# Attention outputs kept turned and unnormalised until the out-projection

## The chip, the cores and the metric

The kernel runs on one NeuronCore of a Trainium2 chip. The metric is the device time of one execution in microseconds. TensorE multiplies into PSUM, VectorE (DVE) and ScalarE (ACT) read PSUM and SBUF, GpSimd (POOL) reads SBUF alone, and DMAs are issued by a queue of an engine, here mostly SyncE's (SP), and carried out by 16 DMA engines.

## The reference

x is (4, 2048, 256) in float32. Attention and feed-forward part read the same normalised x:

```python
xn = _layernorm(x)
q, k = rope(xn @ Wq.T), rope(xn @ Wk.T)       # 16 heads of 16
v = xn @ Wv.T
attn = softmax(where(causal, q @ k.T / 4, min))
x = x + (attn @ v).reshape(B, S, D) @ Wo.T + ffn_fp4(xn)
```

The feed-forward part (SwiGLU with inputs and weights rounded to blockwise FP4) is computed in the first stage and already added to x there; the change doesn't touch it.

## The kernel before

Three stages, each a block of its own with a barrier behind it. `norm_ffn_qkv` (to about 868 us) makes q, k and v and stores them in DRAM; its stores of q and k (line 299) go out by halves of heads:

```python
dst = d["qkp"][p, f // 2, :, ds(g, 1), first:first + HEAD // 2].rearrange("h g e a c -> h (g e a) c")
sp.dma_start(dst, parts[:, p, f, :]).then_inc(parts_stored, 16)   # DRAM: 4 x 32 x 512, bf16
```

`attention` runs 16 iterations, one for each group of four heads (HG) and batch. In an iteration there are four blocks of 512 queries (qb). Each block needs the maximum of every row of scores first: tiles of raw scores in PSUM (`max_tile`, L979; VectorE reduces them, L1143 and L1148), whose maxima GpSimd splits into three bf16 parts, TensorE turns (`max_row`), and SP places as extra rows of q. Then come the scores transposed, keys by queries (`scores`, L1002, with the causal mask as a product with identity, L1007), the exponential on ScalarE (`exponentials`, L1071) and the weighing of v (`weigh`, L1022), four heads side by side in `acc`. v has 32 columns a head (VW), 16 of v and one of ones, so that `acc` holds for each head 16 rows of outputs and a row of sums, turned: channels by queries. When a block is complete ScalarE copies `acc` to `acc_sb` (`take_acc`, L1076). An "out" follows: TensorE turns it with four transposes (`out_turn`, L1032) into a slot of the same ring of four PSUM tiles that the maxima use, VectorE takes reciprocals of the sums (L1172) and multiplies (L1175, `normalise`), and SP stores `ot` to `oscr` (L913).

The order of all this is written out: `ORDER` is a string in which s is a step of scores (weighings follow from them), t a tile of maxima, r a placing of a row, o an out. `attention_plan` makes the list from it, and each engine goes through this list and takes what is its own. Tiles of the next iteration run ahead (about half of them), so every iteration but the last has 140 tiles. The loop has two iterations in its body on SP, TensorE and VectorE, one on ScalarE, which loads its table of functions again at the start of each.

`out_projection` handles 16 groups of 512 rows in pairs. SP loads a group by four DMAs, one for each group of heads (L1240, 128 partitions x 4 x 64 elements); for each tile of 128 rows TensorE turns the outputs (two transposes, L1269), ScalarE copies them to `attT` (L1295), TensorE multiplies with Wo (L1277, float32, two instructions a product) and VectorE adds x (L1311). SP stores a group of y (L1252), behind which the next loads stand in its queue.

Of the kernel before, what the change touches and what calls it, by code (L numbers as in the profile page):

```python
# [26 lines left out]
P = 128  # L27
# [25 lines left out]
OUTW = HG * HEAD  # L53
OT = GT * OUTW

LEAD = 0.52
WEIGH_AT, WEIGH_STEPS = 3, 2
ORDER = ("stsststtsttssststststsssstststsstssrtsssttstssotststsstsststststtstsststssststststssttsstsssstst"
         "stsststsssststssttsotsststsstttsststsststttsstsssststsstttststssssststststssttsssstrtstssttstsst"
         "stsssstssttstssssrtsssttstsststsoststsststststtsststtstsssstsstststttssssssstststtrsststsssststs"  # L60
         "ttssttstsstssstsstttstsststssststsstststtststsssssstttssssto")
# [737 lines left out]
def ring_places(plan, more):  # L799


    uses = [e for e in plan if e[0] in ("tile", "row", "out") and (more or e[0] == "out" or not e[-1])]
    return {e: n for n, e in enumerate(uses)}


def slot_free(it, n, per_iteration, slots):
# [6 lines left out]
    return it * per_iteration + last - per_iteration + 1 + slots  # L813


def attention(nc, d, identf):
# [21 lines left out]
    with ExitStack() as ctx:  # L838
# [18 lines left out]
        acc_sb = sb("acc_sb", [P, GROUP])  # L857
        recip = sb("recip", [P, GT * HG])
        ot = sb("ot", [P, 2, GT * HG, HEAD])
# [17 lines left out]
        dve_links = sem("dve_links")  # L877
# [4 lines left out]
        out_stored = [sem("out_stored0"), sem("out_stored1")]  # L882
        sp_passed = sem("sp_passed2")
# [3 lines left out]
        def _(sp):  # L887
# [20 lines left out]
            def store(it, more, e):  # L908
                n, _ = place(it, more, e)
                qb = e[1]  # L910
                await_on(sp, sp_passed, tile_taken, n + 1 + TILE_SLOTS)
                dst = d["oscr"].rearrange("h g p c -> (h g) p c")[ds(it * QB + qb, 1)]
                sp.dma_start(dst.rearrange("a p c -> (a p) c"),  # L913
                             ot[:, qb % 2].rearrange("p t e -> p (t e)")).then_inc(out_stored[qb % 2], 16)
# [13 lines left out]
            def iteration(it, par, more):  # L928

                last = QB - 1  # L930
                for e in plan:
                    if e[0] == "row" and (more or not e[-1]):
                        place_row(it, (par + e[-1]) % 2, more, e)
                    elif e[0] == "out":
                        store(it, more, e)
# [19 lines left out]

            await_on(sp, sp_passed, out_stored[0], ITERS * QB // 2 * 16 + 1)
# [3 lines left out]
        def _(pe):  # L960
# [66 lines left out]
            def out_turn(it, more, e):  # L1027

                pe.wait_ge(acc_taken, it * QB + e[1] + 2)
                bank = tile_slot(it, more, e)  # L1030
                for t in range(GT):
                    mm = nc.tensor.transpose(bank[:, t * P:(t + 1) * P], acc_sb[:, t * P:(t + 1) * P], identf[:])  # L1032
# [334 lines left out]
```

## Time and profile before

| | us |
|---|---|
| median of 3 runs | 2679.75 (2678.06 to 2680.13) |
| the profiled execution | 2682.65, its span 2680.5 |
| TensorE busy, whole span | 2496.1 (93%) |
| VectorE busy | 2267.2 (85%) |
| ScalarE busy | 1629.3 (61%) |
| GpSimd busy | 80.7 (3%) |
| mean granted TensorE clock | 0.971 |

Busy is the union of an engine's instructions; a product counts until its last result, also while the next one already streams, so shares of TensorE near 100% say that there are no gaps, not that it works at its peak. A clock of 1.00 is 2.4 GHz, 0.5 is 1.2 GHz. Attention fills the span from about 868 to 2594 us, the out-projection the rest.

### The profile page before, as it was taken

What the parts mean: (1) busy time and instruction counts of PE and PEld (TensorE: products, weight loads), DVE (VectorE), ACT (ScalarE), POOL (GpSimd) and SP (SyncE); (2) the same over time, 40 slices, a digit from 0 to 9 for tenths busy, and PEclk for the clock granted to TensorE, in tenths of its full rate; (3) what the DMA queues carried; (4) which work ended last, traced back from release to release, by engine and by line L of the source; (5) the groups of instructions that cost most, each with busy time, mean ns of one, the idle gap of its engine ahead of it and who ended that gap; (6) DMA issues with size and microseconds to landing.
All of it is one profiled execution on the core that took longest, in us unless ns stands there. A gap on an engine that the chain in (4) does not pass through costs nothing. (4 is left out here: it accounts for less than half of the span.)

```text
span 2680.5 us, 55917 instructions
## 1 busy us (share of the span) xinstructions
PE 2496.1 (93%) x14690; PEld 1211.5 (45%) x14690; DVE 2267.2 (85%) x4941; ACT 1629.3 (61%) x3323; POOL 80.7 (3%) x263
## 2 busy tenths in 40 slices
PE   3699999999998699999999999999999999999979
PEld 2355655555555144344344444344444443433337
DVE  6989889998897888889889888988988988988803
ACT  2354454544543067777777777777777777767752
POOL 0000000000000200000000000000000000000000
PEclk8899999999999599999999999999999999999999
DMA  5022112211221402112112022121121121110017
GB/s 182 34 69 70 56 62 70 70 51 68 69 70 55 122 26 64 31 51 65 27 55 63 25 59 58 30 59 41 47 58 33 51 62 28 52 53 6 7 40 215
DMA packets 174760, 157.83 MB, mean 59 GB/s; under 512 B 53360, under 2 KB 153456, under 8 KB 174576
## 3 DMA queue, kind: packets, MB, share of 16 engines
q1 hardware_dynamic: 174576, 155.39, 19.5%
q8 instruction: 114, 1.87, 0.3%
q14 instruction: 70, 0.57, 0.1%
HBM read 95.81 MB, written 58.72 MB: 58 GB/s over the span
## 5 line engine op out<-in xcount | busy, mean ns | idle before, releaser
L1071 ACT ACTIVATE prob<-score 128x512 f32<-128x512 f32 (+3 forms) x2560 | 1158.7, 542 | 494.5 <-PE score L1007 273.1
L1143 DVE TENSOR_REDUCE top<-tile 128x1 f32<-128x512 f32 x1536 | 957.1, 682 | 109.1 <-PE tile L979 102.5
L1002 PE MATMUL score<-qs,ks 99*128 99x512 bf16 (+3 forms) x2560 | 811.6, 351 | 17.1 <-DMA qs<-row 9.9
L979 PE MATMUL tile<-ks,qs 96*128 96x512 bf16 (+3 forms) x2560 | 786.8, 357 | 30.6 <-POOL ks L1095 22.3
L1022 PE MATMUL acc<-prob,vs 128*32 128x512 f32 (+3 forms) x5120 | 537.9, 535 | 0.0
L1148 DVE CUSTOM_DVE_ANT_0 tile<-tile,mask 128x128 f32<-128x128 f32 (+3 forms) x1024 | 471.6, 519 | 59.7 <-PE tile L979 43.6
L1002 PEld LDWEIGHTS score<-qs,ks 99*128 99x128 bf16 x2560 | 246.7, 97 | 405.5 <-ACT prob L1071 204.9
L979 PEld LDWEIGHTS tile<-ks,qs 96*128 96x128 bf16 x2560 | 236.4, 98 | 327.2 <-DVE top L1143 100.9
L361 PE MATMUL gu<-wguT,xT 128*128 128x512 f32 (+1 forms) x768 | 314.4, 563 | 20.4 <-DVE hid L669 20.4
L1022 PEld LDWEIGHTS acc<-prob,vs 128*32 128x32 f32 x5120 | 130.3, 109 | 242.9 <-issue 139.3
L361 PEld LDWEIGHTS gu<-wguT,xT 128*128 128x128 f32 x768 | 145.0, 192 | 167.6 <-issue 124.8
L1007 PE MATMUL score<-identb,maskb 128*128 128x128 bf16 x1024 | 214.5, 221 | 3.4 <-issue 3.4
L397 PE MATMUL misc<-wdT,hT 128*128 128x256 f32 x768 | 183.9, 391 | 1.3 <-ACT hT L462 1.3
L397 PEld LDWEIGHTS misc<-wdT,hT 128*128 128x128 f32 x768 | 147.9, 196 | 32.7 <-issue 11.3
L1148 DVE DVE_READ_ACCUMULATOR2_ANT top<- 128x1 f32 x1024 | 143.4, 140 | 0.0
L385 PE MATMUL misc<-xT,wqkvT_sb 128*128 128x512 f32 x256 | 118.7, 607 | 7.6 <-ACT xT L462 7.6
L1007 PEld LDWEIGHTS score<-identb,maskb 128*128 128x128 bf16 x1024 | 101.2, 99 | 48.0 <-issue 2.5
L467 ACT ACTIVATE magic<-scaled 128x704 f32<-128x704 f32 (+1 forms) x96 | 71.1, 741 | 74.5 <-DVE scaled L125 74.5
L482 ACT ACTIVATE silu<-gu 128x704 f32<-128x704 f32 x64 | 48.5, 757 | 101.7 <-PE gu L361 101.7
L134 DVE SCALAR_TENSOR_TENSOR scaled<-magic,scaled 128x704 f32<-128x704 f32 (+1 forms) x96 | 78.7, 819 | 29.8 <-ACT magic L467 29.2
L462 ACT COPY hT<-misc 128x512 f32<-128x512 f32 (+1 forms) x128 | 58.1, 482 | 64.6 <-PE misc L393 64.0
L393 PE MATMUL misc<-identf_sb,hq 128*128 128x128 f32 x384 | 59.8, 279 | 33.3 <-DVE hq L138 28.0
(101 smaller groups left out, 1758.5 us busy)
## 6 DMA issues: line engine op xcount, KB each, us to landing
qkp<-parts SPq DMA_DIRECT2D x192, 128.0 KB
qs<-qkp SPq DMA_DIRECT2D x384, 64.0 KB, 2.6
ks<-qkp SPq DMA_DIRECT2D x384, 64.0 KB, 2.5
vscr<-vt SPq DMA_DIRECT2D x16, 1024.0 KB, 4.6
vs<-vscr SPq DMA_DIRECT2D x16, 1024.0 KB, 6.2
x_all<-in_x SPq DMA_DIRECT2D x16, 512.0 KB, 8.9
oscr<-ot SPq DMA_DIRECT2D x64, 128.0 KB, 1.7
att<-oscr SPq DMA_DIRECT2D x64, 128.0 KB, 2.7
```

The lines of the kernel that those rows point to most:

```text
L134: link(nc.vector.scalar_tensor_tensor(out=scaled, in0=magic, scalar=1.25 * MAGIC, in1=scaled, op0=ALU.max, op1=ALU.add))
L361: mm = nc.tensor.matmul(gu[:, t % 2, c0:c0 + w], xT[:, KT + k, t * P:(t + 1) * P], wguT[:, k, c0:c0 + w], start=(k == 0), stop=(k == KT - 1))
L385: mm = nc.tensor.matmul(bank, wqkvT[:, k, t * P:(t + 1) * P], xT[:, k, :], start=(k == 0), stop=(k == KT - 1))
L397: mm = nc.tensor.matmul(bank[:, 0:DIM], hT[:, t % 2, i, :], wdT[:, i, :], start=(i == 0), stop=(i == IT - 1))
L467: nc.scalar.activation(magic[:, par, 0:w], scaled[:, par, 0:w], ACT.Abs, scale=MAGIC).then_inc(magic_ready, 1)
L979: mm = nc.tensor.matmul(bank[:, h * width:(h + 1) * width], qs[par][0:ROWS, h0 + h, q0:q0 + P], ks[par][0:ROWS, h0 + h, k0:k0 + width], st ...
L1002: mm = nc.tensor.matmul(bank[:, 0:width], ks[par][0:ROWS_M, h, kb * P:(kb + 1) * P], qs[par][0:ROWS_M, h, qb * GROUP + off:(qb + 1) * GROU ...
L1007: mm = nc.tensor.matmul(bank[:, 0:P], maskb[:], identb[:], start=False, stop=True, skip_group_check=True)
L1022: mm = nc.tensor.matmul(acc[h * VW:(h + 1) * VW, off:GROUP], vs[par][:, kb // GT, kb % GT, h, :], prob[:, (HG * n + h) % PROB_SLOTS, 0:GRO ...
L1071: nc.scalar.activation(prob[:, k % PROB_SLOTS, 0:width], score[:, k % SCORE_SLOTS, 0:width], ACT.Exp, scale=HEAD ** -0.5).then_inc(probs_r ...
L1143: nc.vector.tensor_reduce(top[:, j, h0, c:c + 1], bank, AX.X, ALU.max).then_inc(tile_taken, 1)
L1148: last = nc.vector.tensor_tensor_reduce(out=head, in0=head, in1=mask[:, GROUP - width:GROUP], scale=1.0, scalar=MASK, op0=ALU.add, op1=ALU ...
```

## The change

The outputs of a block stay as `acc` has them, turned and unnormalised. `out_turn` and `normalise` go, and with them the outs' use of the ring. `acc_sb` has two halves; ScalarE waits before its copy until the store of two blocks earlier has landed; SP stores the half to `oscr`, now 128 rows x 512 (per head 16 of outputs, one of sums, 15 unused). `ORDER` is written anew.

In the last iteration, at out 1, SP loads the sums of batches 0 to 2 (twelve DMAs of 16 rows, one for each batch and query block, into 64 partitions x 1536). VectorE takes their reciprocals after its last tile, GpSimd splits them into three bf16 parts, and SP stores the parts to `rscr` before the stage ends. Batch 3 has the same done within the out-projection, during its first groups.

The out-projection loads a group turned: two DMAs by SP, two by ScalarE's queue (`load_att`), and the three parts of the reciprocals, 48 rows (`load_recips`). A product of a 0/1 matrix `pick` with the parts spreads a head's reciprocals over its 16 channels and adds the parts; VectorE multiplies, and TensorE projects without turning anything. The diff, without declarations of tiles and semaphores:

```diff
...
-ORDER = ("stsststtsttssststststsssstststsstssrtsssttstssotststsstsststststtstsststssststststssttsstsssstst"
...
+ORDER = ("stssttsststtssttsstsssstsststsststsssrtststststststostssstststssttststststsststssttsstststssstss"
...
-    uses = [e for e in plan if e[0] in ("tile", "row", "out") and (more or e[0] == "out" or not e[-1])]
+    uses = [e for e in plan if e[0] in ("tile", "row") and (more or not e[-1])]
...
+def load_sums(sp, d, dst, b, loaded):
+    for qb in range(QB):
+        src = d["oscr"][:, b * QB + qb].rearrange("h (k r) c -> h k r c", r=VW)[:, :, HEAD, :]
+        sp.dma_start(dst[qb * HEADS:(qb + 1) * HEADS, :], src).then_inc(loaded, 16)
...
+def split_recips(pool, nc, links, base, rest, parts):
+    nc.gpsimd.tensor_copy(parts[0], rest).then_inc(links, 1)
+    pool.wait_ge(links, base + 1)
+    nc.gpsimd.tensor_tensor(rest, rest, parts[0], ALU.subtract).then_inc(links, 1)
...
+    pool.wait_ge(links, base + 3)
+    return nc.gpsimd.tensor_tensor(parts[2], rest, parts[1], ALU.subtract)
...
-                await_on(sp, sp_passed, tile_taken, n + 1 + TILE_SLOTS)
+                await_on(sp, sp_passed, acc_taken, it * QB + qb + 2)
...
+                sp.dma_start(dst.rearrange("a p c -> (a p) c"), acc_sb[:, qb % 2, :]).then_inc(out_stored[qb % 2], 16)
...
+                        store(it, e)
+                        if more is False and e[1] == 1:
...
+                            for b in range(BATCH - 1):
+                                load_sums(sp, d, sums[:, b, :], b, sums_loaded)
...
+            await_on(sp, sp_passed, recips_split, 1)
+            for p in range(PARTS):
+                sp.dma_start(batch_recips(d, p, slice(0, BATCH - 1)), sum_parts[:, p, :, :]).then_inc(recips_stored, 16)
+            await_on(sp, sp_passed, recips_stored, PARTS * 16)
...
-            def out_turn(it, more, e):
...
-                bank = tile_slot(it, more, e)
-                for t in range(GT):
-                    mm = nc.tensor.transpose(bank[:, t * P:(t + 1) * P], acc_sb[:, t * P:(t + 1) * P], identf[:])
-                mm.then_inc(tile_full, 1)
...
-                nc.scalar.copy(acc_sb[:], acc[:]).then_inc(acc_taken, 1)
+                qb = e[2]
+                act.wait_ge(out_stored[qb % 2], it * (QB // 2 * 16) + qb // 2 * 16 + 1)
+                nc.scalar.copy(acc_sb[:, qb % 2, :], acc[:]).then_inc(acc_taken, 1)
...
-            def normalise(it, more, e):
...
-                link(nc.vector.reciprocal(recip[:], sums[:, :, HEAD]))
...
-                nc.vector.tensor_tensor(ot[:, qb % 2], sums[:, :, 0:HEAD],
-                                        recip[:].unsqueeze(2).broadcast_to([P, GT * HG, HEAD]),
-                                        ALU.mult).then_inc(tile_taken, 1)
...
+            dve.wait_ge(sums_loaded, (BATCH - 1) * QB * 16)
+            nc.vector.reciprocal(sums[:], sums[:]).then_inc(recips_ready, 1)
...
+        def load_recips(eng, g):
+            b, qb = g // QB, g % QB
+            eng.dma_start(recips[g % 2][:], d["rscr"][:, b, qb]).then_inc(recips_loaded[g % 2], 16)
+        def load_att(eng, g, k):
+            for h in range(HGS // KT):
+                src = d["oscr"][k * HGS // KT + h, g].rearrange("(k r) c -> k r c", r=VW)[:, 0:HEAD, :]
+                rows = slice(h * HG * HEAD, (h + 1) * HG * HEAD)
+                eng.dma_start(attT[g % 2][rows, k, :], src).then_inc(att_loaded[g % 2], 16)
...
+            for g in range(2):
+                load_recips(sp, g)
+                load_att(sp, g, 0)
+            load_sums(sp, d, sums[:], BATCH - 1, sums_loaded)
+            for g in range(GROUPS):
+                if g == 1:
+                    sp.wait_ge(recips_split, 1)
+                    for p in range(PARTS):
+                        sp.dma_start(batch_recips(d, p, slice(BATCH - 1, BATCH)).rearrange("p b c -> p (b c)"),
+                                     sum_parts[:, p, :]).then_inc(recips_stored, 16)
+                if g + 2 < GROUPS:
+                    sp.wait_ge(spread_full, (g + 1) * KT)
+                    if g + 2 == LAST:
+                        sp.wait_ge(recips_stored, PARTS * 16)
+                    load_recips(sp, g + 2)
+                    sp.wait_ge(scaled_ready, (g + 1) * KT)
+                    load_att(sp, g + 2, 0)
+                sp.wait_ge(prod_taken, (g + 1) * GT)
+                sp.dma_start(rows[g], y[g % 2][:]).then_inc(y_stored[g % 2], 16)
+            for stored in y_stored:
+                sp.wait_ge(stored, GROUPS // 2 * 16)
+        @block.scalar
+        def _(act):
+            act.dma_start(pick[:], d["spread"]).then_inc(pick_loaded, 16)
+            for g in range(2):
+                load_att(act, g, 1)
+            for g in range(GROUPS - 2):
+                act.wait_ge(scaled_ready, (g + 1) * KT)
+                load_att(act, g + 2, 1)
...
+            def spread_recips(g):
+                pe.wait_ge(recips_loaded[g % 2], (g // 2 + 1) * 16)
...
+                    pe.wait_ge(scaled_ready, (g - 1) * KT)
                 for k in range(KT):
...
+                    nc.tensor.matmul(spread[:, g % 2, k, :], pickb[:, k * P:(k + 1) * P], recips[g % 2][:],
+                                     start=True, stop=True).then_inc(spread_full, 1)
...
+            def project(g, t):
+                pe.wait_ge(scaled_ready, (g + 1) * KT)
+                if g:
+                    pe.wait_ge(prod_taken, (g - 1) * GT + t + 1)
                 for k in range(KT):
-                    mm = nc.tensor.matmul(prod[:, t % 2, 0:DIM], attT[:, t % 2, k * P:(k + 1) * P], woT[:, k, :],
+                    mm = nc.tensor.matmul(prod[:, t, 0:DIM], scaledT[g % 2][:, k, t * P:(t + 1) * P], woT[:, k, :],
                                           start=(k == 0), stop=(k == KT - 1))
                 mm.then_inc(prod_full, 1)
...
+            spread_recips(0)
+            for g in range(GROUPS):
+                if g + 1 < GROUPS:
+                    spread_recips(g + 1)
+                for t in range(GT):
+                    project(g, t)
...
+            def scale(g):
+                dve.wait_ge(att_loaded[g % 2], (g // 2 + 1) * HGS * 16)
+                if g >= 2:
+                    dve.wait_ge(prod_full, (g - 1) * GT)
+                for k in range(KT):
+                    dve.wait_ge(spread_full, g * KT + k + 1)
+                    nc.vector.tensor_tensor(scaledT[g % 2][:, k, :], attT[g % 2][:, k, :], spread[:, g % 2, k, :],
+                                            ALU.mult).then_inc(scaled_ready, 1)
+            scale(0)
+            for g in range(GROUPS):
+                if g + 1 < GROUPS:
+                    scale(g + 1)
...
+                    dve.wait_ge(sums_loaded, QB * 16)
+                    nc.vector.reciprocal(sums[:], sums[:]).then_inc(recips_ready, 1)
...
+                for t in range(GT):
+                    dve.wait_ge(prod_full, g * GT + t + 1)
+                    nc.vector.tensor_tensor(y[g % 2][:, t, :], prod[:, t, 0:DIM], x_all[:, g * GT + t, :],
                                             ALU.add).then_inc(prod_taken, 1)
...
-    d["oscr"] = nc.dram_tensor("oscr", [HGS, GROUPS, P, OT], F32).ap()
+    d["oscr"] = nc.dram_tensor("oscr", [HGS, GROUPS, P, GROUP], F32).ap()
+    d["rscr"] = nc.dram_tensor("rscr", [PARTS, BATCH, QB, HEADS, GROUP], BF16).ap()
...
```

Where the instructions now stand, at two places. TensorE at the end of an iteration, before: the last weighing, a tile, the four transposes of out 3, and the next iteration's first score.

```order
L1022 MATMUL acc<-prob,vs 32x256 x4
L1019 REGISTER_ALU
L1022 MATMUL acc<-prob,vs 32x128 x4
L965 REGISTER_ALU
L979 MATMUL tile<-ks,qs 128x512
L1029 REGISTER_ALU
L965 REGISTER_ALU
L1032 MATMUL tile<-identf_sb,acc_sb 128x128 x4
L996 ISA
L1000 ISA
L1002 MATMUL score<-qs,ks 128x512
L1007 MATMUL score<-identb,maskb 128x128
```

After, the same place:

```order
L1002 REGISTER_ALU
L1016 MATMUL tile<-ks,qs 128x512
L1059 MATMUL acc<-prob,vs 32x256 x4
L1056 REGISTER_ALU
L1059 MATMUL acc<-prob,vs 32x128 x4
L1033 ISA
L1037 ISA
L1039 MATMUL score<-qs,ks 128x512
L1044 MATMUL score<-identb,maskb 128x128
L1002 ISA
L1016 MATMUL tile<-ks,qs 128x512
```

The out is gone, the tile that stood behind the weighing stands ahead of it, and the first score comes directly behind the weighing. Behind these rows come score, score, tile, tile and score; the last is the fourth of the iteration (score 3).

The queue of SP in the out-projection, one group, before and after:

```order
L1240 DMA att<-oscr 128x4x64
L1240 ISA
L1240 DMA att<-oscr 128x4x64
L1252 ISA
L1252 DMA out<-y 128x4x256
L86 REGISTER_ALU
L1240 ISA
L1240 DMA att<-oscr 128x4x64
```

```order
L822 DMA last_sums<-oscr 16x1x512 x4
L1262 DMA recips<-rscr 48x1x512
L1268 DMA attT<-oscr 64x1x512 x2
L1292 DMA out<-y 128x4x256
L1281 DMA rscr<-last_parts 64x512 x3
L1262 DMA recips<-rscr 48x1x512
L1268 DMA attT<-oscr 64x1x512 x2
L1292 DMA out<-y 128x4x256
```

The loads were 128 partitions x 4 x 64 elements, four a group. Now SP has two of 64 partitions x 512 (ScalarE's queue has the other two), ahead of them the parts of the reciprocals, and once the last batch's sums and parts.

## Rows read from the trace of the kernel before

**Rows 1.** Busy time of one iteration: stretch, length, engines, clock.

```profile
1352.69:1455.62 102.93, 102.05 (x725) 42.56 (x724) 92.06 (x241) 75.65 (x166) 4.05 (x16) 1.00 0.17 48
```

**Rows 2.** Groups of two iterations: busy, mean ns | idle before.

```profile
L1032 PE MATMUL tile<-identf_sb,acc_sb 128*128 128x128 f32 x32 | 4.9, 275 | 0.9 <-ACT acc_sb L1076 0.9
...
L1175 DVE TENSOR_TENSOR ot<-tile,recip 128x256 f32<-128x256 f32 x8 | 3.4, 424 | 0.6
```

**Rows 3.** Timeline around an out within an iteration.

```profile
1467.98 0.60 PE L1002 MATMUL score<-qs,ks 99*128 99x512 bf16 x2
...
1468.42 0.60 PE L1032 MATMUL tile<-identf_sb,acc_sb 128*128 128x128 f32 x4
...
1468.86 0.38 PE L979 MATMUL tile<-ks,qs 96*128 96x512 bf16 x1
```

**Rows 4.** Timeline where one iteration ends and the next begins.

```profile
1454.64 0.91 PE L1022 MATMUL acc<-prob,vs 128*32 128x256 f32 x16
...
1455.48 0.39 PE L979 MATMUL tile<-ks,qs 96*128 96x512 bf16 x1
1455.62 0.59 ACT L1076 COPY acc_sb<-acc 128x512 f32<-128x512 f32 x1 [0.55 <-PE acc L1022]
1456.22 1.28 ACT L1071 ACT_TABLE_LOAD   x1
...
1456.33 0.65 PE L1032 MATMUL tile<-identf_sb,acc_sb 128*128 128x128 f32 x4 [0.46 <-ACT acc_sb L1076]
...
1456.82 0.38 PE L1002 MATMUL score<-qs,ks 99*128 99x512 bf16 x1
...
1457.52 4.26 ACT L1071 ACTIVATE prob<-score 128x512 f32<-128x512 f32 x10
...
1458.17 0.39 PE L1002 MATMUL score<-qs,ks 99*128 99x512 bf16 x1
```

**Rows 5.** Timeline from attention to the out-projection.

```profile
2592.25 0.34 SPq L913 DMA_DIRECT2D oscr<-ot  x1
2594.26 13.71 SPq L1240 DMA_DIRECT2D att<-oscr  x12
...
2599.09 1.11 PE L1269 MATMUL o_turned<-identf_sb,att 128*128 128x128 f32 x4 [7.75 <-DMA att<-oscr]
```

**Rows 6.** Groups of VectorE after 2546 us.

```profile
L1172 DVE RECIPROCAL recip<-tile 128x16 f32<-128x16 f32 x2 | 0.5, 257 | 45.9 <-PE tile L1032 45.9
```

**Rows 7.** Chain of waits, out-projection: start, length, what.

```profile
2600.31 2.07 PE o_prod L1277 x4
...
2649.60 1.13 PE o_prod L1277 x4
2650.95 0.87 PE o_prod L1277 x4
...
2658.85 1.13 PE o_prod L1277 x4
```

**Rows 8.** DMA issues of the whole run: KB each, us to landing.

```profile
qkp<-parts SPq DMA_DIRECT2D x192, 128.0 KB
...
att<-oscr SPq DMA_DIRECT2D x64, 128.0 KB, 2.7
out<-y SPq DMA_DIRECT2D x16, 512.0 KB, 3.2
```

**Rows 9.** Stretches as in rows 1, with DMA share and GB/s last.

```profile
328.00:339.00 11.00, 10.26 (x43) 6.60 (x42) 10.41 (x10) 5.53 (x10) 0.00 (x0) 1.00 0.27 87
315.25:316.75 1.50, 1.10 (x9) 0.87 (x9) 1.47 (x3) 0.65 (x2) 0.00 (x0) 1.00 1.04 392
2620.00:2660.00 40.00, 38.41 (x208) 32.22 (x207) 14.45 (x34) 12.18 (x34) 0.00 (x0) 1.00 0.81 223
```

**Rows 10.** Groups of VectorE over the whole run.

```profile
L125 DVE SCALAR_TENSOR_TENSOR scaled<-xn,inv 128x512 f32<-128x512 f32 x32 | 22.1, 692 | 1.1
...
L105 DVE RECIPROCAL inv<-inv 128x96 f32<-128x96 f32 (+2 forms) x3 | 2.1, 702 | 0.1
```

## What was predicted, before the changed kernel had run

> **What bounds the kernel now.** I read the page first, then the attention stage cut into single iterations, then the places where TensorE does not go from one matmul straight into the next, and last the out-projection and the DMA queues.
>
> An iteration of attention is 102.9 us, of which TensorE is busy 102.05, VectorE 92.06 and ScalarE 75.65, at full clock [rows 1]. What TensorE does there it does back to back; the reader is to see that the other two have 10 and 27 us of slack. So in attention a microsecond less on TensorE is a microsecond gained, unless the slack of the others is used up at just that place, and time saved on VectorE alone is worth nothing.
>
> The out-projection goes by TensorE as well. The same product comes again 9.25 us later, from 2649.60 to 2658.85 [rows 7], for eight tiles: eight times 0.87 of products [rows 7] and 0.22 of turning (half of rows 3's 0.44), and a gap of 0.5 at the loop's edge. That is 4.63 us a group. VectorE and ScalarE mostly wait. The DMA engines are busy 0.81 of that stretch at 223 GB/s [rows 9], so they are close behind. This is the number I come back to.
>
> **The turning products in attention.** Each out has four transposes. Within an iteration (outs 0, 1, 2) the transposes begin at 1468.42 and the next tile's product at 1468.86, and the row ahead, with two products in 0.44, runs straight into them [rows 3]. So an out costs TensorE 0.44 us. There are 48 such outs; in the last iteration there are no tiles for a next one and ScalarE's exponentials set the pace when out 2 comes, so 47 count: 47 x 0.44 = 20.7 us. The row of the group, 32 transposes in 4.9 us [rows 2], would give 0.61 an out, but it contains the drain that the next product overlaps.
>
> Out 3, at the iteration's end, costs more. The tile's product at 1455.48 is over at 1455.70, the transposes wait for ScalarE's copy until 1456.33, and the next iteration's first score begins at 1456.82: 1.12 us [rows 4]. I do not count this as gained. Behind the copy ScalarE loads its table (1.28) and gives the first exponential at 1457.52; score 3 needs the slot that this one frees, and begins at 1458.17, which is 3.53 after the weighing began at 1454.64 [rows 4]. ScalarE's string of copy, table load and exponential hangs on the weighing alone and stays as it is. In the new order one tile has moved ahead of the weighing, and score 3 has six pieces ahead of it: three scores with masks (0.28 each) and three tiles (0.22 each), 1.5 us, behind 0.84 of weighing. TensorE would be ready for score 3 at 2.34 after the weighing's start and can't begin until 3.53: 1.19 us of waiting where 1.12 went away. Value: 0; bounds: 15 x 1.12 = 16.8 us gained (the wait is filled), or 5 us lost (it costs a little more at each end).
>
> VectorE loses 64 reciprocals and 64 multiplications of 0.42 us each [rows 2]. It was not the bound, so 0. The tile slots come free earlier and the ring loses its use by outs; both only help, and TensorE waits for a slot almost nowhere. The rest of the order is nearly the old one with neighbours exchanged; I give it 0, with 5 us to both sides. ScalarE's new wait, for the store of two blocks earlier, is met tens of microseconds before. Attention: -20.7 us, from -38 to -10.
>
> **The bulk of reciprocals, batches 0 to 2.** SP issues twelve small loads of sums at out 1 of the last iteration; nothing but the last placing of a row stands behind them in its queue within the next 15 us. VectorE's last tile work is long done: it stands idle 45.9 us around the last two outs [rows 6]. A reciprocal of 96 elements takes 0.70 us [rows 10], so 1536 take about 16 times that, 11 us, and GpSimd's four passes over 64 x 1536 follow. No row shows such a pass; SP asks for their result only when attention ends, so all four together may take 25 us or more before one microsecond shows. Cost 0; if that cover went, 10 us. Three stores of the parts stand behind the last store of outputs, at 0.34 an issue or a bit more, where the transposes, reciprocal and multiplication of the last out went: from -1 to +2, I take +0.5.
>
> **The out-projection, by engines.** TensorE: four tiles x 0.87, and two spreading products of 512 columns at 0.22 each [rows 3] make 3.92 a group against 4.63. VectorE: two multiplications of 128 x 512 at 0.69 [rows 10] and four sums of 0.42, 3.1. ScalarE only issues. By engines alone the stage gets 16 x 0.7 = 11 us shorter.
>
> **The out-projection, by DMA.** This decides. Before, a load of a group is `128x4x64` on the SBUF side, 128 partitions and 512 rows in DRAM, and the stretch at 0.81 of 16 engines shows all of them at work [rows 9]. Now one load takes 16 of each 32 rows of four heads: in DRAM it is 4 blocks x 16 rows x 2 KB. The program has DMAs of this kind: the stores of q and k, 4 blocks x 32 rows in DRAM from 128 partitions, 128 KB each [rows 8]. While they run alone one after the other, the DMA share is 0.27, that is 4.3 of 16 engines, at 87 GB/s; 1.5 us of the store of v, over all engines, show 1.04 and 392 GB/s [rows 9]. Eight stores one behind the other never reach 0.5, so they all queue on the same four. I take it that a DMA with four blocks on one side uses four engines, the same four each time, on whichever side the four stands.
>
> Then the sum per group is: four loads of 128 KB, 1.34 us each at 98 GB/s (four of sixteen at the full rate of 392) or 1.51 at the 87 of q's stores: 5.4 to 6.0, taken 5.7. The parts of the reciprocals, 48 KB: 0 to 0.9, taken 0.6. The store of y, 512 KB over all sixteen at 392 GB/s, takes 1.35 of these four as well. Together 7.65 us a group on the four engines, from 7.2 to 8.3, against 4.63 before: the queue of the four replaces TensorE as the bound. Two groups of loads are under way at a time and a landed group is multiplied in 1.4 us, so the four never run dry.
>
> Whole stage, from its first load issued: 1.9 us until data flows (an issue of 0.6 and half of a load's 2.7 [rows 8]), 16 x 6.3 for loads, 14 x 1.35 for the stores that come before the last load, 1 for sums and last parts, 0.7 to land: 123.3. Behind the last load stand two multiplications (1.4), four tiles (3.5), a sum, an issue and a landing of 3.2 [rows 8] (4.2 together): 132.4. Before, it was 2680.5 - 2594.3 = 86.2 [rows 5]. So +46, taken +47 since the last tiles may run at the lower clock, as the first did (2.07 for a tile at 2600.31, [rows 7]). Bounds +41 and +58. The last batch's reciprocals (3.7 us on VectorE) lie under the wait for loads.
>
> The Trainium skill, "DMA: Bandwidth & Descriptors", section "Why a DMA increments its semaphore by 16 and not by 1", says that a DMA is split over the largest number up to 16 that divides the slowest dimension of both its sides, on the lowest-numbered engines. By that rule the new loads (4 and 64) get four engines and those of the parts (3 and 48) three, which would add 2 us to the sum. For stores the trace agrees (4 and 128, share 0.27); that a four on the reading side does the same, no row here shows. Without the rule one could hold that the reader's side is free, and that is the second rival's case.
>
> **Sum.** The profiled execution took 2682.65, its span 2680.5; the median of the timed runs is 2679.75, 2.9 below. 2682.65 - 20.7 + 0.5 + 47 = 2709.4, and 2.9 less: 2706.5, predicted 2707.
>
> **Rivals.** (1) The loads spread over all engines, since only the DRAM side read has a four. Then the engines' sum holds, 3.9 a group, a store and its next load of parts fit into it, and the stage ends 11 us sooner less 1 for the later start: 2679.75 - 20.7 + 0.5 - 10 = 2650, faster. For it: 0.81 of share now and fewer, longer packets. Against it: q's stores. It decides at a period under 4.63. (2) The four engines are the bound at their fast end, and the gap at the iteration's end closes too, because the new order fills it: -37.5 and +43 give 2686. For it: the order was written anew. Against it: score 3 stands six pieces behind the weighing. (3) TensorE, now idle half of each group, runs at its lower clock through the stage: 1.74 a tile and 0.85 for spreading are 7.8 a group, so the period is TensorE's again, and the last group costs 3.5 more: 2712. For it: after the idle 7.75 us before the stage [rows 5] the first tile took 2.07. Against it: half busy is not idle.
>
> **Numbers.** Forecast 0.68, rival 1 0.12, rival 2 0.08, rival 3 0.12. The forecast's own range is 2690 to 2722. Low is 2684, where rival 2 ends; high is 2726: slow end of the loads and -10 in attention. Rival 1 stays outside. A change within 0.2% (5.4 us) can't be told from none. Faster 0.14 (rival 1 and an edge of rival 2), same 0.05, slower 0.81.
>
> **What would show it.** In the profile after: a DMA share of 0.3 to 0.5 in the out-projection, a period of 7.4 to 8.2 us a group, TensorE waiting for scaledT and VectorE for attT's loads; no L1032, iterations of some 101.6 us, and a wait of about 1.2 us of the fourth score at an iteration's start. Wrong: a period under 5 us there (the spread is not by four), or iterations under 100.8 (the gap did close) or over 102.9.

## The result: slower by 0.4%, direction right, size wrong

The median of seven runs is 2690.5 us (2687.7 to 2693.3) against 2680.1 for the kernel before in the same comparison: ratio 1.0038, 95% interval 1.0029 to 1.0048, slower by 10 us. The forecast was slower by 27, to 2707; the measured time lies inside the range of 2684 to 2726. In the profiled executions (spans of 2688.7 and 2680.5) two large numbers nearly cancel, and both were mis-sized:

| part | forecast, us | measured, us |
|---|---|---|
| up to the first load of the out-projection | -20.2 | -32.4 |
| out-projection, from its first load issued | +46 to +47 | +40.6 |
| sum | +26.8 | +8.2 |

They are read so: the first load of the out-projection is issued at 2561.89 after and was at 2594.26 before [rows 5]; from there to the end it is 126.8 us against 86.2. Of the 18.6 us between the two sums, 12.2 are attention's and 6.4 the out-projection's.

### The profile page after: what moved, and what is told of

Same layout as the page of the kernel before. It is cut to its first block and busy times, and to the rows that moved or that the text cites. A ratio compares the mean times of both kernels' runs of the same rounds, so it can differ in the third digit from the quotient of the medians.

```text
span 2688.7 us, 54370 instructions
## 1 busy us (share of the span) xinstructions
PE 2464.2 (92%) x14338; PEld 1180.0 (44%) x14338; DVE 2256.6 (84%) x4848; ACT 1601.6 (60%) x3259; POOL 93.3 (3%) x271
## 5 line engine op out<-in xcount | busy, mean ns | idle before, releaser
L1039 PE MATMUL score<-qs,ks 99*128 99x512 bf16 (+3 forms) x2560 | 813.4, 350 | 31.5 <-ACT prob L1098 16.5
L1016 PE MATMUL tile<-ks,qs 96*128 96x512 bf16 (+3 forms) x2560 | 776.6, 355 | 30.9 <-POOL ks L1124 22.3
L1059 PE MATMUL acc<-prob,vs 128*32 128x512 f32 (+3 forms) x5120 | 535.4, 536 | 0.0
L1039 PEld LDWEIGHTS score<-qs,ks 99*128 99x128 bf16 x2560 | 244.3, 97 | 446.4 <-ACT prob L1098 250.3
L1059 PEld LDWEIGHTS acc<-prob,vs 128*32 128x32 f32 x5120 | 133.6, 109 | 244.0 <-issue 135.5
L395 PEld LDWEIGHTS misc<-wdT,hT 128*128 128x128 f32 x768 | 148.5, 197 | 32.8 <-issue 11.3
```

Of the source, the lines that this page charges most:

```text
L395: mm = nc.tensor.matmul(bank[:, 0:DIM], hT[:, t % 2, i, :], wdT[:, i, :], start=(i == 0), stop=(i == IT - 1))
L1016: mm = nc.tensor.matmul(bank[:, h * width:(h + 1) * width], qs[par][0:ROWS, h0 + h, q0:q0 + P], ks[par][0:ROWS, h0 + h, k0:k0 + width], st ...
L1039: mm = nc.tensor.matmul(bank[:, 0:width], ks[par][0:ROWS_M, h, kb * P:(kb + 1) * P], qs[par][0:ROWS_M, h, qb * GROUP + off:(qb + 1) * GROU ...
L1059: mm = nc.tensor.matmul(acc[h * VW:(h + 1) * VW, off:GROUP], vs[par][:, kb // GT, kb % GT, h, :], prob[:, (HG * n + h) % PROB_SLOTS, 0:GRO ...
```

## The profile after

Two stretches after: an iteration (it answers to [rows 1]) and eight groups of the out-projection (length, engines, clock, DMA share, GB/s).

```profile
1346.58:1447.28 100.70, 99.53 (x709) 40.86 (x710) 89.59 (x233) 75.41 (x166) 4.04 (x16) 1.00 0.18 54
2603.59:2660.64 57.05, 39.04 (x144) 27.84 (x144) 20.92 (x48) 0.00 (x0) 0.00 (x0) 0.91 0.42 154
```

An iteration takes 100.70 us where it took 102.93; over twelve of them the means are 100.69 and 102.66, 1.97 less, and 1.3 was forecast. The eight groups take 57.05 us, 7.13 each, at a DMA share of 0.42. That is the picture of the forecast (0.3 to 0.5), with a period just under its 7.2 to 8.3. The rows before had 0.81 and 223 GB/s [rows 9].

The end of an iteration, timeline after (start, length, engine, line; in brackets the idle time before and what ended it). L1059 is the weighing, L1039 the score, L1105 ScalarE's copy. It answers to [rows 4].

```profile
1446.35 0.86 PE L1059 MATMUL acc<-prob,vs 128*32 128x256 f32 x16
...
1447.14 0.39 PE L1039 MATMUL score<-qs,ks 99*128 99x512 bf16 x1
...
1447.28 0.58 ACT L1105 COPY acc_sb<-acc 128x512 f32<-128x512 f32 x1 [0.71 <-PE acc L1059]
...
1447.88 1.28 ACT L1098 ACT_TABLE_LOAD   x1
...
1449.18 2.06 ACT L1098 ACTIVATE prob<-score 128x512 f32<-128x512 f32 x4
...
1449.83 0.39 PE L1039 MATMUL score<-qs,ks 99*128 99x512 bf16 x1 [1.03 <-ACT prob L1098]
```

Here the forecast holds. The first exponential comes 2.83 us after the weighing began (2.88 before), and TensorE now waits 1.03 us at the fourth score where the transposes and their gap had been; 1.19 was forecast.

SyncE between attention and the out-projection, and then the two waits that matter in the eight groups (total us, times, longest):

```profile
2556.38 0.34 SPq L941 DMA_DIRECT2D oscr<-acc_sb  x1
2556.83 2.00 SPq L991 DMA_DIRECT2D rscr<-sum_parts  x3
2561.89 0.75 SPq L1262 DMA_DIRECT2D recips<-rscr  x1
```

```profile
DVE scaledT L1352 <- DMA attT<-oscr: 30.3, 7, 5.9
...
PE o_spread L1314 <- DMA recips<-rscr: 17.2, 8, 3.0
```

From the last store of outputs to the first load it was 2.0 us before [rows 5]; it is 5.5 now, since the stores of the parts have to land too. VectorE's multiplications for four groups and the last one:

```profile
2643.59 1.28 DVE L1352 TENSOR_TENSOR scaledT<-attT,o_spread 128x512 f32<-128x512 f32 x2 [3.43 <-DMA attT<-oscr]
...
2651.79 1.29 DVE L1352 TENSOR_TENSOR scaledT<-attT,o_spread 128x512 f32<-128x512 f32 x2 [5.58 <-DMA attT<-oscr]
...
2658.00 1.28 DVE L1352 TENSOR_TENSOR scaledT<-attT,o_spread 128x512 f32<-128x512 f32 x2 [3.59 <-DMA attT<-oscr]
...
2666.76 1.29 DVE L1352 TENSOR_TENSOR scaledT<-attT,o_spread 128x512 f32<-128x512 f32 x2 [6.15 <-DMA attT<-oscr]
...
2679.38 1.29 DVE L1352 TENSOR_TENSOR scaledT<-attT,o_spread 128x512 f32<-128x512 f32 x2 [4.59 <-PE o_prod L1322]
```

The first four come 8.2, 6.2 and 8.8 us apart, each released by a load of attT. Two groups' loads are in the queues at a time, which could give the alternation; that was not tried. From the first multiplication (2570.81) to the last (2679.38) it is 7.24 us a group, and 9.3 us follow. Head and tail are as the sum had them; the 5.6 us that the stage is shorter than the sum's 132.4 are 15 periods of 7.24 in place of 7.65.

## Experiments on attention

**The new table alone, and the turns alone.** Two kernels fill the square of table and turns. The edit of the first, made to the kernel after; the second is the same exchange made to the kernel before:

```diff
-ORDER = ("stssttsststssttsstsssstsststsststsssr...   # table of after
+ORDER = ("stsststtsttssststststsssstststsstssrt...   # table of before
```

> The kernel after with the ORDER table of the kernel before, everything else as after. Theory A (order): in the old table one pair of weighings (steps 12 and 13) has three tiles between its halves, in the new one none has; every break behind a weighing costs TensorE about 0.42 us of drain and 0.10 at the entry, 0.52 an iteration. So iterations become 101.2 us against 100.69, and the kernel is slower than after by 16 x 0.52 = 8 us, about 2698. Rival B (the extra gain of attention comes from the removed turns alone, at the iteration's end): iterations stay within 0.1 us of 100.69 and the time within 2 us of 2690. Rival C (entry into the unrolled last-but-one iteration): the iteration before the last one, 104.6 us in after and 112.0 in before, goes back to about 112 with the old table, which adds 7 us more, whatever the others do.

> The kernel before with the ORDER table of the kernel after: turns, normalising and the old out-projection stay. It is the fourth corner to before (102.66 us an iteration), after (100.69) and the kernel after with the old table (102.20). Theory E (the old table had put the turning products where TensorE would wait for ScalarE's exponentials anyway, the new one puts tiles there): with both the new table and the turns nothing hides the turns any more, so they cost their full 4 x 0.44, less what the wait of the fourth score at the iteration's start (1.03) then covers: 100.69 + 1.3 to 1.7 = 102.0 to 102.4 us an iteration. The new table is then worth some 0.4 us an iteration with turns and 1.5 without. Time 2680 - 15 x 0.4 = 2674. Rival F (the new table is simply better by 1.5 us an iteration, whatever stands in it): 101.2 us, 2657. Rival G (each table fits its own kernel alone): over 102.7, slower than before.

Measured, mean of twelve iterations and median of the runs:

| | old table | new table |
|---|---|---|
| with turns | 102.66 us; 2680 | 103.07 us; 2687.0 |
| without turns | 102.20 us; 2715.1 | 100.69 us; 2690.5 |

The new table is worth 24.6 us without turns, and costs 4 to 6 with them (ratio to before 1.0016, 1.0007 to 1.0025; rival G: each table fits its own kernel). The turns alone, with the table left as it was, give 0.46 us an iteration, not 1.3. One iteration of each:

```profile
1353.36:1455.55 102.19, 100.82 (x709) 40.52 (x708) 89.73 (x233) 75.53 (x165) 4.03 (x16) 1.00 0.18 53
```

```profile
1357.03:1460.22 103.19, 101.89 (x726) 42.82 (x725) 91.97 (x241) 76.02 (x165) 4.00 (x16) 1.00 0.17 47
```

Theories A, B, E and F fall by size or sign. C does too: the last but one iteration rises by 2.3 us to 106.9, 0.8 more than the others do, not to 112. Where the old table loses its gain is seen in the timeline of the first kernel, some 64 us into an iteration, where out 2 used to stand. ACT is ScalarE's exponentials, PEld the weight load of a score:

```profile
1414.63 3.54 ACT L1098 ACTIVATE prob<-score 128x512 f32<-128x512 f32 x7
...
1414.79 0.39 PE L1039 MATMUL score<-qs,ks 99*128 99x512 bf16 x1
...
1415.28 0.10 PEld L1039 LDWEIGHTS score<-qs,ks 99*128 99x128 bf16 x1 [0.31 <-ACT prob L1098]
...
1415.77 0.10 PEld L1039 LDWEIGHTS score<-qs,ks 99*128 99x128 bf16 x1 [0.31 <-ACT prob L1098]
...
1416.26 0.10 PEld L1039 LDWEIGHTS score<-qs,ks 99*128 99x128 bf16 x1 [0.39 <-ACT prob L1098]
```

Seven exponentials follow one another with no gap in 3.54 us, about 0.5 each, and the weight load of each score waits until one of them has freed the slot (0.31, 0.31, 0.39). TensorE itself loses less than these waits, since it streams a tile meanwhile: a score and a tile come every 0.49 us here, and every 0.44 at the same place before, behind the transposes. ScalarE sets the pace there. The transposes of 0.44 had stood in that time; taken out, part of them comes back as waiting.

How much comes back is read by setting the starts of TensorE's matmuls in the two kernels with the old table side by side, one by one, the transposes left out. At each of outs 0, 1 and 2 the kernel without turns gains 0.44 and has lost 0.37, 0.34 and 0.35 of it again (mean of twelve iterations) before the next out's place: 1.05 of the 1.3 removed come back. The other half of the 0.46 comes at an iteration's start. With the old table and turns every second iteration is 0.53 longer, 102.92 against 102.39, because TensorE also stops at the edge of the loop. One of the short ones, and the stop at the start of the long one behind it:

```profile
1455.62:1558.01 102.39, 101.78 (x725) 42.40 (x724) 91.93 (x241) 75.56 (x166) 4.04 (x16) 1.00 0.17 48
```

```profile
1559.62 0.39 PE L1002 MATMUL score<-qs,ks 99*128 99x512 bf16 x1 [0.25 <-issue]
```

Without turns all take 102.20: the wait at the fourth score covers the edge, and 0.41 is gained there in every second iteration, nothing in the others.

What the new table does better by 1.51 us an iteration can be placed in part. Added up over four iterations, the time that TensorE spends beyond streaming between a score or a tile and what follows it is 8.3 us an iteration with the old table and 6.9 with the new one; from the first weighing matmul of a group to what follows the last it is 32.2 in both. So it is in the waits for slots, not in the breaks around weighings. Which exchange of letters gives it was not tried.

**Is the split pair of weighings the cause?** In the old table three tiles stand between weighings 12 and 13. In the kernel before:

```diff
-"stsststsssststssttsotsststsstttsststsststtt...
+"stsststsssststssttsotsststssstttststsststtt...
```

> The kernel before with five letters of its ORDER exchanged: weighings 12 and 13 stand next to each other and the three tiles that stood between them come behind. Theory A: 0.52 us less an iteration, 102.1 in place of 102.66, and 8 us less in all, about 2672. Rival B: nothing, within 2 us of 2680. Rival D: VectorE gets three tiles at once behind the pair and TensorE waits for a tile slot there, which gives half or all of it back: 2676 to 2680.

2685.7 us, ratio 1.0019 (1.0010 to 1.0028) to before: slower, by 0.48 us an iteration. Theory A falls, and so do B and D as they were stated: none had it slower. D named the wait that is seen. TensorE, by its rows at that place, waits for VectorE at the tiles:

```profile
1393.04 0.39 PE L979 MATMUL tile<-ks,qs 96*128 96x512 bf16 x1 [0.18 <-DVE top L1143]
1393.64 0.39 PE L979 MATMUL tile<-ks,qs 96*128 96x512 bf16 x1 [0.21 <-DVE top L1143]
```

Here a break behind a weighing is cheaper than three tiles in a row, which need slots that VectorE has not yet freed.

**ScalarE's copy at the iteration's end.** The kernel after, the last block's copy moved:

```diff
 # ScalarE
-elif e[0] == "weigh" and e[1] == last_step[e[2]]:
+elif e[0] == "weigh" and e[1] == last_step[e[2]] and e[2] < QB - 1:
 # VectorE
+if e[0] == "weigh" and e[1] == last_step[QB - 1]: take_last_acc(it, e)
```

> The kernel after, but the copy of an iteration's last block of outputs is made by VectorE, not by ScalarE; the other three blocks stay with ScalarE. Theory A (the fourth score of an iteration waits 1.03 us for ScalarE's string of copy 0.58, table load 1.28 and first exponential, which begins only when the last weighing is done): without the copy the table load no longer waits for the weighing, the first exponential comes as soon as the first score is there, the wait falls to 0.2 us or less, and an iteration takes 99.8 us: 15 x 0.85 = 13 us less than after, about 2677. Rival B (VectorE, 90 us busy an iteration, has tiles queued there, and its copy of 0.7 us and its wait for the weighing make TensorE wait for tile slots): half or all of it comes back, 2683 to 2692. Rival C (the wait at the fourth score isn't ScalarE's string): no change of the iteration, 2690.

Iterations fell to 99.94 us, 0.75 less (theory A had 0.85). Yet the kernel took 2698.9, 8.4 more than after: in the last iteration VectorE's bulk reciprocals stood behind the copy, and so behind the last weighing. Timeline of that kernel (VectorE, GpSimd, SyncE's stores of the parts):

```profile
2542.13 0.69 DVE L1201 COPY acc_sb<-acc 128x512 f32<-128x512 f32 x1 [44.70 <-PE acc L1059]
2542.74 9.73 DVE L1228 RECIPROCAL sums<-sums 64x1536 f32<-64x1536 f32 x1
...
2552.54 1.46 POOL L833 CAST sum_parts<-sums 64x1536 bf16<-64x1536 f32 x1 [59.60 <-DVE sums L1228]
...
2558.76 3.08 POOL L839 TENSOR_TENSOR sum_parts<-sums,sum_parts 64x1536 bf16<-64x1536 f32 x1
2561.93 1.34 SPq L991 DMA_DIRECT2D rscr<-sum_parts  x2
```

That is the cover of which the prediction said "if that cover went, 10 us". Bare, it is 9.73 for the reciprocals and 9.3 for four passes of GpSimd, 19 in all: the prediction's 10 left GpSimd out. Next, the copy moved behind the reciprocals, in the last iteration alone:

> As the run with the last block's copy on VectorE, but in the last iteration VectorE makes the bulk reciprocals first, while it is idle, and the copy behind them. Theory A (the copy on VectorE saves 0.75 us an iteration, and the time was lost again because the bulk reciprocals of 9.7 us and GpSimd's four passes of 9.3 us came to stand behind the last weighing): iterations stay at 99.9 us, the first load of the out-projection is issued some 6 us after the last score as in after, and the time is 2690.5 - 11.5 = 2679. Rival B (something else in that kernel holds the end up): over 2690.

2678.7 us, 11.8 less than after and no different from before (ratio 0.9993, 0.9984 to 1.0003). Its iteration; TensorE is now busy all but 0.2 us of it:

```profile
1342.59:1442.53 99.94, 99.73 (x712) 41.10 (x711) 89.98 (x235) 74.97 (x165) 4.02 (x16) 1.00 0.19 54
```

**Is it the copies behind which ScalarE is late?** The old table without turns, and all four copies on VectorE:

> The kernel after with the old ORDER table, and all four copies of an iteration's blocks of outputs made by VectorE in place of ScalarE (in the last iteration the last one behind the bulk reciprocals). With the old table and the copies on ScalarE an iteration took 102.20 us, and TensorE waited 0.28, 0.36 and 0.28 us for exponentials some 2.6 us behind each of ScalarE's three inner copies, where the turning products used to stand, and 1.0 us at the fourth score. Theory E (the removed turns had stood in time that TensorE would have waited for ScalarE, behind its copy of 0.59; without them the wait shows): the copies off ScalarE, these waits go, and the iteration falls by 0.7 to 0.9 for the inner copies and 0.75 for the last, to 100.6 to 100.8 us; the kernel to 2715.1 - 22 = 2693. Rival H (the waits behind the turns' places are ScalarE's pace over the whole stretch, whatever copies): only the last copy's 0.75 comes, 101.45 us, 2704. Rival B (VectorE's tiles are late by the copies and TensorE waits for slots): over 101.5.

2699.8 us, iterations of 101.56. Rival H was nearest (101.45). The 1.0 at the fourth score went. Set beside the kernel with the old table and ScalarE's copies, it loses as much at the place of out 1, 0.07 more at out 2 and 0.11 less at out 0: ScalarE's exponentials pace those stretches, not its copies. A tile at 4.2 us of the iteration now waits 0.2.

```profile
1349.12:1450.60 101.48, 101.21 (x712) 40.84 (x711) 91.49 (x237) 73.78 (x161) 4.03 (x16) 1.00 0.19 54
```

## Experiments on the out-projection

**All loads over 16 engines, and attT's alone.** In the kernel after:

```diff
-src = ...rearrange("(k r) c -> k r c", r=VW)[:, 0:HEAD, :]
+src = ...rearrange("(k r) c -> r k c", r=VW)[0:HEAD]
-d["rscr"][:, b, qb]
+d["rscr"][:, b, qb].rearrange("p h c -> h p c")
 # rows of woT, of the spreading matrix: permuted to match
```

> The kernel after with the loads of attT and of the reciprocals' parts written so that the slowest dimension on the DRAM side is 16 in place of 4 and 3; the channels come in another order within a block of 64, and the rows of woT and of the spreading matrix are laid out to match. The bytes, packets and instructions are the same. Theory A (four engines are the bound of the out-projection): the DMA share there rises to about 0.6, the period of a group falls from 7.12 us to TensorE's 4.4 (16 products of 0.22 and two spreading ones of 0.44), the stage from 126.8 to about 83 us, the kernel to about 2646. Rival B (the chain through SP's queue is the bound: store of y, load of parts, spreading, multiplication, next load): the period stays over 6.3 us and the kernel above 2675. Rival C (TensorE at its lower clock): the period is about 7.8 and nothing is gained.

> As the run with both loads changed, but the loads of the reciprocals' parts stay with 3 on the slowest side. Theory A: 48 KB on three engines take about 0.5 us and no longer stand behind attT's loads there, so the stage is 0 to 8 us longer than with both changed, the kernel 2646 to 2654. Rival B (the spreading products wait for the parts' load, 17 us in 60 us of the stage in after): the stage gains less than half of what both changes give, above 2668.

2652.0 us (ratio 0.9892, 0.9876 to 0.9907) and 2660.5. Seven groups of the first:

```profile
2591.76:2622.40 30.64, 28.96 (x126) 21.40 (x126) 19.25 (x42) 0.00 (x0) 0.00 (x0) 1.00 0.83 249
```

4.38 us a group at a share of 0.83 and 249 GB/s: the same bytes in the same number of loads, and the bound is gone. Theory A holds; B and C fall. With attT's loads alone the period is 4.85 (six groups):

```profile
2594.03:2623.14 29.11, 25.31 (x108) 18.41 (x108) 17.13 (x36) 0.00 (x0) 0.00 (x0) 1.00 0.78 227
```

Its 2660.5 us lie between what its theory A (2646 to 2654) and rival B (above 2668) expected: the parts, left in their old form, cost 8.5 us there. With both changed the stage takes 89.9 us, not 83. From the first spreading product to the first tile's product it is 0.53 (0.44 was taken for the two) and from there to the next spreading 3.65 where nothing waits, so TensorE's floor is 4.18 and the mean of 4.38 has 0.2 of waiting in it; the stage's start and a pause of SyncE (below) cost the rest.

**What the four engines charge.** Each load of attT issued a second time into a tile nobody reads (one line more in `load_att`, and twice the count in VectorE's wait):

> The kernel after, but in the out-projection each load of attT is issued a second time into a spare tile that nothing reads, and the multiplication waits for both: it prices 512 KB in this form, a group's loads. Theory A (four engines bound the stage, and 512 KB cost them 5.7 us as the prediction took from the stores of q and k): the period of a group goes from 7.1 to 12.8 us, the time to 2690 + 16 x 5.7 = 2781. Variant A2 (the four engines are quicker on 2 KB packets, 5.0 us for 512 KB): the period becomes 12.1, the time 2770. Rival B (the chain through SP's queue is the bound in after and the loads have slack): the period goes up by less than 3 us, to 10, and the time to 2735 or less.

```profile
2614.96:2713.61 98.65, 53.66 (x144) 36.32 (x144) 20.91 (x48) 0.00 (x0) 0.00 (x0) 0.72 0.35 132
```

Eight groups in 98.65 us, 12.33 each, against 7.13: 512 KB cost 5.20 us, 101 GB/s, a quarter of the 392 in [rows 9] within 3%. The median is 2772.3. The loads are the bound, at a price nearer to A2's than to A's 5.7.

**The parts alone over 16 engines:** the second edit of the diff above, without the first.

> The kernel after, but the loads of the reciprocals' parts have 16 heads as their slowest dimension in place of 3 parts; attT's loads stay with four. Theory A (what counts is the sum on the four engines): 48 KB leave three of them, 0.5 us a group, and the time falls by 0 to 8 us, to 2682 to 2690. Rival B (a load of parts that is spread over 16 engines has its pieces on the four busy ones behind attT's loads all the same, and lands no sooner): no change, within 2 us of 2690.

```profile
2602.63:2657.43 54.80, 40.34 (x144) 28.82 (x142) 21.75 (x48) 0.00 (x0) 0.00 (x0) 0.88 0.45 161
```

6.85 us a group, 0.28 less, and 2685.7 us, 4.8 less. Spreading the parts, a quarter of which then still falls to the four engines, gives 0.3 a group; 0.6 was taken for all of them.

**Both gains together:** loads over 16 engines, the last copy on VectorE, the bulk reciprocals ahead of it in the last iteration.

> The same with the loads of attT and of the parts spread over 16 engines (16 as the slowest dimension on the DRAM side, woT's and the spreading matrix's rows laid out to match). The two gains lie in different stages and add: 2690.5 - 11.5 - 38.5 = 2640 to 2641, 1.5% faster than the kernel before. Rival B (the earlier end of attention collides with nothing, but the stage's start is set by something else): above 2648.

2640.6 us, ratio 0.985 (0.9834 to 0.9867): 1.5% faster than the kernel before, and the sum of the two gains to a microsecond.

## Why the prediction was right in sign and wrong in size

- **The change makes the out-projection slower because its loads use four engines: right, and shown.** Four on the DRAM side alone is enough: with 16 there, the same bytes in as many loads, the period falls from 7.13 to 4.38 (4.85 with attT's loads alone), and 512 KB more cost 5.20, which is a quarter of the full rate. That was the inference from the stores of q and k. The Trainium skill, "DMA: Bandwidth & Descriptors", section "Why a DMA increments its semaphore by 16 and not by 1", says that the slowest dimensions of both sides set the number of engines; these runs agree for the side that is read.
- **The term of loads was mis-sized.** 5.7 a group for attT was 5.20 when measured; 0.6 was taken for the parts, and spreading them gave 0.28. I took the middle between 98 and 87 GB/s, and the loads doubled ran at 101. The two terms together were up to 0.8 a group too high, but the period is only 0.4 to 0.5 below 7.65 (7.24 on the mean, 7.13 in the eight groups). So what is left of it, which the sum had as 1.35 for the store of y, comes to some 1.6 by difference; no run took it apart. The three together are the 6 us of the out-projection.
- **"The rest of the order is nearly the old one with neighbours exchanged; I give it 0": the step that failed most.** By the last copies (2590.04 before, 2580.68 with the old table and no turns, 2555.71 after) the turns alone gave -9.4 and the table -25.0; the forecast had -20.7 and 0. The three copies, in that order:

```profile
2590.04 0.59 ACT L1076 COPY acc_sb<-acc 128x512 f32<-128x512 f32 x1 [0.54 <-PE acc L1022]
```

```profile
2580.68 0.59 ACT L1105 COPY acc_sb<-acc 128x512 f32<-128x512 f32 x1 [0.55 <-PE acc L1059]
```

```profile
2555.71 0.59 ACT L1105 COPY acc_sb<-acc 128x512 f32<-128x512 f32 x1 [0.55 <-PE acc L1059]
```

That the time still fell inside the range of 2684 to 2726 is partly luck: the 25.0 left out and the 11.3 too much for the turns have opposite signs.
- **"What TensorE does there it does back to back": wrong where outs 0 to 2 stand.** 102.05 of 102.93 busy [rows 1] doesn't say that TensorE sets the pace. Its busy time includes matmuls whose ends overlap the next wait, and at those places ScalarE would have held it up 0.34 to 0.37 us, had the transposes not been there.
- **The iteration's end counted as 0: right but for the loop's edge.** 1.03 us of waiting took the place of 1.12, and with the copy off ScalarE 0.75 came out. In every second iteration 0.41 was gained, since the wait now covers the edge of the loop as well: 0.2 on the mean, some 3 us, within the bounds given.
- **A term that was missing: entry into the written-out iterations.** The last but one iteration took 112.0 us before and 104.6 after. TensorE stopped before, with nothing to wait for, and went on at half speed (a score of 512 columns took 0.63 us in place of 0.38); the row, then two stretches of before and the first of after:

```profile
2384.18 0.27 PE L1007 MATMUL score<-identb,maskb 128*128 128x128 bf16 x1 [3.37 <-issue]
```

```profile
2379.23:2389.00 9.77, 5.94 (x22) 2.73 (x22) 4.61 (x10) 4.68 (x7) 0.00 (x0) 0.73 0.28 76
2389.00:2399.00 10.00, 10.00 (x81) 5.01 (x79) 8.88 (x19) 7.38 (x19) 1.01 (x4) 0.92 0.39 126
```

```profile
2353.53:2363.30 9.77, 8.71 (x65) 4.07 (x63) 8.47 (x19) 8.14 (x20) 1.01 (x4) 1.00 0.29 82
```

All three kernels with turns have this stop of 2.8 to 3.4 us at this place, whichever table they have, and none of those without. The last but one iteration is 106.9 us with the old table and no turns, 5.05 less where the others are 0.46 less, so 4.6 of the 9.4 us are this and not the work removed. (The other 4.8 are 14 iterations of 0.46, less 1.5 that the last iteration became longer.) The profile says of the stop only "issue": TensorE waited for nothing that it shows. But it has a DMA queue of the kind "instruction", and within each of the three stops a 16 KB packet of it is under way and done 1.3 to 1.5 us before TensorE goes on. Before, from 2380.5 to 2384.2:

```profile
q8 instruction: 1, 0.02, 1.6%
```

In after such a packet comes at 2354.07, while TensorE works. So a late load of TensorE's own instructions is the likely cause; it was argued from the rows, not tried. Nor is after free of stops: its last but one iteration is 3.9 us longer than the others, with VectorE stopped for 2.0 us and TensorE waiting for it:

```profile
DVE top L1178 <- issue: 2.0, 1, 2.0
```

With the old table and all copies on VectorE neither stop is there, and that iteration takes 101.4 us.
- **The boundary:** +0.5 was forecast. From the last copy to the first load it was 4.22 us and is 6.18: +2.0.

In the ledger: -9.4 (turns, 4.6 of it the entry) - 25.0 (table) + 2.0 (boundary), +40.6 for the stage, make +8.2, the difference of the spans. The two profiled executions also began attention 1.1 us apart; the other runs, with the same first stage, began it 938.3 to 941.4 us into theirs, so that is spread.

## What to carry to other kernels

A busy engine is the bound only where nobody would stop it if it were quicker: before counting removed work as gained, take it out of the timeline on paper and see whether the slot or the operand it reaches next is there, at each place apart. Where a change comes with a new order of work, price order and change in a square of four kernels, not one by one. And read a DMA's slowest dimension on both sides: the same bytes in 16 rows by 4 in place of 4 by 16 made a stage 37 us shorter.

## What the runs showed that I had not expected

- SyncE pauses once in the written-out loop of the out-projection, between the store of the eleventh group and the next load, with all it waits for long met:

```profile
2654.81 3.29 issue
```

It is there at the same group in every kernel of this form (3.8 and 2.9 us with both loads and with attT's alone over 16 engines) but the one with each load twice, whose loop has more instructions: 0.04 us there. A packet of an "instruction" queue lands within it, 1.2 us before SyncE goes on, as in TensorE's stops above. That it is the cause was not tried.
- Behind two spreading products of 48x512 the first f32 tile starts 0.53 us after the first of them, not 0.44 (their busy time of 0.60 includes the last one's drain, as the 0.60 of two scores in [rows 3] does). The rows of the kernel with all loads over 16 engines (store of y, spreading, store, next tiles):

```profile
2618.32 0.38 SPq L1292 DMA_DIRECT2D out<-y  x1
...
2622.38 0.60 PE L1314 MATMUL o_spread<-recips,pickb 48*128 48x512 bf16 x2 [0.47 <-DVE y L1366]
2622.40 0.38 SPq L1292 DMA_DIRECT2D out<-y  x1
2622.91 1.16 PEld L1322 LDWEIGHTS o_prod<-woT_sb,scaledT 128*128 128x128 f32 x6 [0.42 <-issue]
```

- A period of the stage is 7.13 us with TensorE's clock granted at 0.91, busy 0.68 of the time with waits of 1.3 to 3.0 us between groups, and 12.33 us at a clock of 0.72, with waits of 5.2 to 6.2. In neither case was TensorE the bound.
- GpSimd's casts of 64x1536 took 1.46 us and its subtractions 3.08.
